# GpSimd's low parts moved, VectorE's first passes reordered, and two loops written out

## The reference

```python
# cross attention: 32 query heads, 8 key/value heads, head size 128
kv = concatenate([context, latents], axis=1)            # 256 rows per batch row
q, k, v = latents @ Wq, kv @ Wk, kv @ Wv                # q and k get an RMS norm per head
probs = softmax(q @ k.T / sqrt(128))
x = x + tanh(g_xattn[0]) * ((probs @ v) @ Wo)
# feed-forward, INTER = 1376, on layernorm(x) / 128
inter = silu(xf @ w_gate.T) * (xf @ w_up.T)
inter_q = trunc(clip(inter * 128, -128, 127))
x = x + tanh(g_ffn[0]) * trunc(clip((inter_q @ w_down.T) * 128, -128, 127))
```

## Time and profile before

| what | value |
| --- | --- |
| median of 3 runs | 1199.65 us (1199.49 to 1199.93) |
| the profiled execution | 1198.55 us, of which its span is 1196.8 us |
| TensorE busy (matmuls) | 1176.8 us, 98% |
| VectorE, ScalarE, GpSimd busy | 830.3, 580.5 and 326.9 us |
| TensorE clock granted | 1.000 over the span |

### The profile page before, as it was taken

How to read it: one execution, slowest core, us unless ns; L and a number is a source line. 1 busy time by engine, 2 the same in 40 slices (tenths; PEclk the granted TensorE clock), 3 DMA queues, 4 the chain that set the end, 5 groups by cost and what they waited for, 6 DMA issues and landing times.

```text
span 1196.8 us, 20842 instructions
## 1 busy us (share of the span) xinstructions
PE 1176.8 (98%) x6979; PEld 1008.7 (84%) x6979; DVE 830.3 (69%) x2402; ACT 580.5 (49%) x1352; POOL 326.9 (27%) x286
## 2 busy tenths in 40 slices
PE   8999999999999999999999999999999999999998
PEld 7888888888888888888988888888787777778786
DVE  6867677666766766667666667668877887875355
ACT  5645455454545455454554545554444445543432
POOL 4513022221303212031231203122342412225542
PEclk9999999999999999999999999999999999999999
DMA  7001010000101010010000000002122212583316
GB/s 281 12 25 54 1 37 18 36 33 2 53 0 35 18 35 35 0 53 0 35 19 33 35 0 0 1 1 56 32 80 79 81 54 71 204 321 100 108 44 246
DMA packets 36266, 69.65 MB, mean 58 GB/s; under 512 B 5858, under 2 KB 22242, under 8 KB 34166
## 3 DMA queue, kind: packets, MB, share of 16 engines
q1 hardware_dynamic: 30726, 56.65, 13.7%
q0 software_dynamic: 3760, 8.40, 2.2%
q10 hardware_dynamic: 1728, 3.93, 0.8%
HBM read 60.57 MB, written 12.32 MB: 61 GB/s over the span
## 4 chain that ended last, share of the span: by engine, by line
PE 60%; DVE 21%; issue 9%; ACT 5%; POOL 2%; DMA 2%; SPq 1%; DVEq 0%; ACTq 0%; POOLq 0%
PE bank L414 14%; PE bank L416 14%; PE bank L415 14%; PE bank L2274 5%; PE bank L2123 3%; DVE probs L1276 3%; ACT probs L881 2%; PE bank L1951 2%; PE bank L2286 2%; DVE iq L1475 2%; DVE k_junk L1231 2%; DVE row_max L1249 2%; DVE pt_lo L1263 2%; POOL k_rstd L648 1%; PE bank L1893 1%
## 5 line engine op out<-in xcount | busy, mean ns | idle before, releaser
L881 ACT ACTIVATE probs<-bank,exp_bias,q_rstd 128x256 f32<-128x256 f32 x256 | 141.1, 562 | 135.7 <-DVE exp_bias L1257 135.7
L1268 DVE TENSOR_TENSOR o_lo<-bank,o_hi 128x512 fp32r<-128x512 f32 x64 | 44.2, 691 | 175.6 <-ACT o_hi L874 175.6
L414 PE MATMUL bank<-wkv_hi,kv_src_lo 128*128 128x256 f32 x512 | 145.0, 283 | 0.7 <-DVE kv_src_lo L1318 0.7
L416 PE MATMUL bank<-wkv_hi,kv_src_hi 128*128 128x256 f32 x512 | 145.0, 283 | 0.0
L415 PE MATMUL bank<-wkv_lo,kv_src_hi 128*128 128x256 f32 x512 | 144.9, 283 | 0.0
L652 POOL TENSOR_TENSOR q_rstd<-q_var,minus_half 128x8 f32<-128x8 f32 x32 | 52.4, 1637 | 299.0 <-DVE q_var L1236 299.0
L870 ACT ACTIVATE pt_hi<-bank 128x512 fp32r<-128x512 f32 x128 | 69.6, 596 | 116.1 <-PE bank L1951 114.4
L414 PE MATMUL bank<-wo_hi,o_lo 128*128 128x512 f32 x256 | 104.2, 407 | 1.6 <-DVE o_lo L1268 1.2
L414 PE MATMUL bank<-wq_hi,kv_src_lo 128*128 128x512 f32 x256 | 103.2, 403 | 0.6 <-DVE k_lo L1218 0.6
L416 PE MATMUL bank<-wo_hi,o_hi 128*128 128x512 f32 x256 | 101.5, 396 | 0.0
L415 PE MATMUL bank<-wo_lo,o_hi 128*128 128x512 f32 x256 | 101.0, 394 | 0.0
(11 more groups left out here) (300 smaller groups left out, 3079.2 us busy)
## 6 DMA issues: line engine op xcount, KB each, us to landing
weights<-r_w SPq DMA_DIRECT2D x16, 768.0 KB, 9.7
wq_raw<-wq SPq DMA_DIRECT2D x8, 1024.0 KB, 4.8
wo_raw<-wo SPq DMA_DIRECT2D x8, 1024.0 KB, 4.8
wkv_raw<-wkv SPq DMA_DIRECT2D x8, 512.0 KB, 3.3
gu_raw<-w_gate SPq DMA_DIRECT2D x10, 256.0 KB, 3.4
gu_raw<-w_up SPq DMA_DIRECT2D x10, 256.0 KB, 3.7
wd_raw<-w_down SPq DMA_DIRECT2D x10, 256.0 KB, 3.8
y_back<-y_dram SPq DMA_DIRECT2D x5, 512.0 KB, 9.0
```

The costliest lines, as they stand in the source:

```text
L414: eng.matmul(out_ap, a_lo, b_hi, start=start, stop=False)
L416: return eng.matmul(out_ap, a_hi, b_hi, start=False, stop=stop)
L881: act.activation(probs[:, h, :], scores_ps[h // 2][:, (h % 2) * 256:(h % 2) * 256 + 256], ACT.Exp, bias=exp_bias[:, h:h + 1], scale=q_rstd ...
L1268: dve.tensor_tensor(o_lo[:, par, :], o_ps[:, :], o_hi[:, par, :].bitcast(F32), ALU.subtract)\
```

## The change

ScalarE's `wkv_high` of pass 5 stands ahead of the exponentials. GpSimd's `wkv_low` waits in addition for the bias of pass 5. GpSimd's `gu_low` is cut into two instructions, each for one of the two weights, and these and `wd_low` wait for steps of VectorE's work on the chunks; the counts of `gu_lo_ready` double, and SyncE drops one wait in its loop that the other covers. In the second pass of group 0 VectorE's order changes. `groups` and `chunks` are Python loops now, so every pass and chunk is written out.

```diff
--- before.py
+++ after.py
@@ -445,20 +445,14 @@
 
         def groups(eng, one_group):
 
-            one_group(0)
-            with eng.Fori(1, G - 1) as g:
+            for g in range(G):
                 one_group(g)
-            one_group(G - 1)
 
         def chunks(eng, one_chunk):
 
 
-            for j in range(2):
-                one_chunk(j, j, P, P)
-            with eng.Fori(1, (CH - 3) // 2) as i:
-                for j in range(2):
-                    one_chunk(i * 2 + j, j, P, P)
-            one_chunk(CH - 3, 0, P, P)
+            for c in range(CH - 2):
+                one_chunk(c, c % 2, P, P)
             one_chunk(CH - 2, 1, P, TAIL)
             one_chunk(CH - 1, 0, TAIL, 0)
 
@@ -531,10 +525,9 @@
             with sp.Fori(1, (CH - 1) // 2) as i:
                 for j in range(2):
                     c = i * 2 + j
-                    sp.wait_ge(gu_lo_ready, c - 1)
                     sp.wait_ge(wd_lo_ready, c - 1)
                     load_chunk(c, j, P)
-            sp.wait_ge(gu_lo_ready, CH - 2)
+            sp.wait_ge(gu_lo_ready, 2 * (CH - 2))
             sp.wait_ge(wd_lo_ready, CH - 2)
             load_chunk(CH - 1, 0, TAIL)
 
@@ -551,7 +544,7 @@
 
             load_context(0)
             load_context(1)
-            sp.wait_ge(gu_lo_ready, CH)
+            sp.wait_ge(gu_lo_ready, 2 * CH)
             sp.wait_ge(wd_lo_ready, CH)
             for e in range(SHARED):
                 sp.dma_start(s_raw[:, e, :], s_w[e, :, :]).then_inc(s_loaded, 16)
@@ -688,6 +681,7 @@
                     if before_end(g, b, 2) and not (isinstance(g, int) and g == 0 and b == 0):
                         k_root(next_pair)
                     if b == 4 and before_end(g, b, 4):
+                        pool.wait_ge(bias_ready, g * NB + 6)
                         wkv_low(g + 1)
                     if before_end(g, b, 2):
                         q_root(next_pair, (b // 2 + 1) % 2)
@@ -695,12 +689,10 @@
             groups(pool, one_group)
 
 
-            def gu_low(c, j, width):
+            def gu_low(c, j, i, width):
                 pool.wait_ge(gu_hi_ready, c + 1)
-                pool.tensor_tensor(gu_lo[:, j, :, :, 0:width].rearrange("p a c n -> p (a c) n"),
-                                   gu_raw[:, j, :, :, 0:width].rearrange("p a c n -> p (a c) n"),
-                                   gu_hi[:, j, :, :, 0:width].bitcast(F32).rearrange("p a c n -> p (a c) n"),
-                                   ALU.subtract).then_inc(gu_lo_ready, 1)
+                pool.tensor_tensor(gu_lo[:, j, i, :, 0:width], gu_raw[:, j, i, :, 0:width],
+                                   gu_hi[:, j, i, :, 0:width].bitcast(F32), ALU.subtract).then_inc(gu_lo_ready, 1)
 
             def wd_low(c, j, width):
                 pool.wait_ge(wd_hi_ready, c + 1)
@@ -711,13 +703,19 @@
 
             def next_low(c, j, width, following):
                 if following:
-                    gu_low(c + 1, 1 - j, following)
+                    if after_first(c):
+                        pool.wait_ge(iq_ready, c * 2)
+                    gu_low(c + 1, 1 - j, 0, following)
+                    pool.wait_ge(inter_step, c * 8 + 1)
+                    gu_low(c + 1, 1 - j, 1, following)
+                    pool.wait_ge(iq_ready, c * 2 + 1)
                     wd_low(c + 1, 1 - j, following)
 
             for t in range(3):
                 ln_root(NB + t)
             pool.wait_ge(probs_ready, 4 * (G * NB - 1))
-            gu_low(0, 0, P)
+            gu_low(0, 0, 0, P)
+            gu_low(0, 0, 1, P)
             routing_maps()
             for t in range(3, NB):
                 ln_root(NB + t)
@@ -939,13 +937,13 @@
                     if isinstance(g, int) and g == 0 and b == 1:
                         key_source_high(6)
                         key_source_high(7)
+                    if b == 5 and before_end(g, b, 3):
+                        wkv_high(g + 1)
                     exps(n, b)
                     if isinstance(g, int) and g == 0 and b == 1:
                         q_copy(next_pair)
                     if prev:
                         o_high(n - 1, (b - 1) % 2)
-                    if b == 5 and before_end(g, b, 3):
-                        wkv_high(g + 1)
                     if b % 2 == 0 and before_end(g, b, 2):
                         for half in range(2):
                             kv_high(next_pair, half, par)
@@ -1350,16 +1348,16 @@
                     if after_start(g, b, 3):
                         add_y(n - 3, (b - 3) % NB)
                     if isinstance(g, int) and g == 0 and b == 1:
-                        k_low(next_pair, par)
                         maxima(n)
                         bias_of(n, b)
+                        k_low(next_pair, par)
+                        pt_low(n - 1)
                         low_pair(3)
-                        pt_low(n - 1)
                         normalise(n)
                         q_norm(next_pair)
-                        o_low(n - 1, (b - 1) % 2)
                         for half in range(2):
                             q_low(next_pair, half, par)
+                        o_low(n - 1, (b - 1) % 2)
                         continue
                     maxima(n)
                     if after_start(g, b, 1):
@@ -2074,7 +2072,7 @@
 
             def inner_chunk(c, j, width, following):
                 if after_first(c):
-                    pe.wait_ge(gu_lo_ready, c + 1)
+                    pe.wait_ge(gu_lo_ready, c * 2 + 2)
                     inner_half(c, j, width, 0)
                 else:
                     pe.wait_ge(ln_lo_ready[0], 2 * NB)
@@ -2104,6 +2102,7 @@
             turn_x(5)
             inner_part_of(0, 0, P, 0, 0, 1, KC)
             turn_x(6)
+            pe.wait_ge(gu_lo_ready, 2)
             inner_part_of(0, 0, P, 0, 1, 0, 1)
             turn_x(7)
             inner_part_of(0, 0, P, 0, 1, 1, KC)
```

## The result

The changed kernel takes 1188.25 us (median of 4 runs, 1188.16 to 1188.85), the one before 1199.57 us in the same comparison (4 runs, 1198.79 to 1199.93): a ratio of 0.9905, interval 0.9889 to 0.992, so 9.6 to 13.3 us less. In a second comparison it was 1189.11 against 1199.99 us, ratio 0.9909 (0.9896 to 0.9923). The forecast was 1190.0 with a range from 1188.3 to 1193.2; the median lies 0.05 us under that range, and the forecast of 9.7 us less became 11.3 by these medians.

A forecast was written before the change was run, and what follows sets the result against it. TensorE, busy 98% of the span, was taken as the bound, so only its gaps could be won back. 6.2 + 1.0 + 2.7 - 0.2 = 9.7 us off the median 1199.65 gave 1190.0 us, range 1188.3 to 1193.2.

The forecast's parts named there:

- Passes b = 6: Attention loop: moving `wkv_hi` and `wkv_lo` earlier removes TensorE's 0.90 us stall in each of seven passes, 6.2 us gained.
- (b): Rival, attention: the stall in b = 6 stays in part; 1193.1 us with half won, 1196.2 with none; chance 0.10.
- (e): Rival, whole kernel: nothing moves, since another chain stands behind each of these waits; 1199 us, chance 0.03.
- Second pass of group 0: Start of attention: VectorE's new order lets TensorE start the scores earlier, 1.0 us gained, ends -0.8 and 2.0.
- Chunks: First feed-forward: VectorE's chunk falls from 11.5 to 10.3 us, under TensorE's 10.88; 2.7 us net gained.
- (a): Rival, chunks: TensorE waits for the new `gu_lo` as long as it waited for VectorE; 1192.6 us, chance 0.14.
- (c): Rival, chunks: the three GpSimd pieces block VectorE for their full length, making the kernel slower; 1208 us, chance 0.03.
- First `gu_lo` in two: Ahead of the chunks: two halves end slightly later and a VectorE bias may wait 0.25 us longer; 0.2 us lost.
- Loops: Attention and chunk loops written out: neither jump nor code fetching shows on TensorE's path; counted 0, ends ±0.3 us a group.
- (d): Rival, attention groups: fetching written-out code stalls TensorE 0.3 us a group over six groups; 1191.8 us, chance 0.03.
- I take the gain over to the median: Last step: the gain summed on the profiled execution (1198.55 us) is subtracted unchanged from the median, 1199.65 - 9.7 = 1190.0 us.

The follow-up runs named there:

- the late half: The changed kernel with the second half of `gu_lo` released by this chunk's first `iq`, about 3.3 us later than by the clip: 1199.31 us.

## Why the prediction was wrong, and where it was right

The mechanisms of the three moves were right, and the sum of their sizes was not: the step that failed is "6.2 + 1.0 + 2.7 - 0.2 = 9.7 us" with nothing for the loops. The stages gave 10.47 us. The largest error is VectorE's order in the second pass of group 0, put at 1.0 and measured at 1.31 us. Term by term:

*Passes b = 6*: 6.2 us predicted, 6.2 measured (0.82 + 0.88 + 5 x 0.90). The times within the pass came too: scaling expected at 304.86, found at 304.76 on the old scale; `q_lo` at 308.1 and 308.13. ScalarE's move alone does it, by the experiment. GpSimd's wait had no term of its own in the sum, and nothing is what it was worth. Rivals (b) and (e) are refuted.

*Second pass of group 0*: 1.0 predicted, 1.31 measured. The start of the second q tile was right (44.2, found 44.06 plus the 0.14 us by which this pass starts earlier), so was that of the values (47.05, found 46.91 plus 0.14). On the old scale the scores came at 50.57 and not 50.85. `q_lo` starts 1.32 us earlier and not 1.03: 0.6 us for `o_lo`, as said, and 0.7 because VectorE reaches the scaling that much earlier (46.51 plus 0.14, against 47.36), where the prediction left 0.4. VectorE no longer idles 0.56 us for `k_hi`. It is a size of a term.

*Chunks*: 2.7 predicted, 2.87 measured. VectorE's chunk was put at 10.3 us and is 10.2 (10.46 less 0.26 of waiting). Its three pieces cost 1.25 us where I had 1.35. The 0.2 us of loss in chunk 2 did not come: chunks 1, 2 and 3 start at 857.56, 868.44 and 879.32. Against the other profiles of before's chunks the gain is up to 3.2 us. Rival (a) is refuted for this order, but the late half shows that it is one step away. Rival (c) fell with the multiply at 906.82, undisturbed beside `gu_lo`. The Trainium skill, "SBUF — State Buffer", section "Who interferes with whom", says that a VectorE instruction with at most one SBUF input, outside the two-port modes, does not contend with GpSimd; that row agrees (one input from PSUM, 0.69 us). The same section of the Trainium skill has `tensor_scalar` able to enter a two-port mode and then contend; the clip at 907.54 is one, and it takes 0.67 us instead of 0.43 and ends 0.28 us after `gu_lo`.

*First `gu_lo` in two*: -0.2 predicted, about -0.1 measured, by the mechanism that was named. The last bias is held for 0.77 to 0.80 us in every profile with two halves and for 0.63 to 0.65 in every one with a single piece, and except in the run that reorders VectorE there, TensorE's pass in which it lies takes 6.75 to 6.78 us against 6.61 to 6.66.

*Loops*: 0 predicted. In the whole change they are worth 0.2 us (10.47 against 10.28), inside the stated ends. It lies in the last group, in the pass with the wait for `x_sb`: 9.25 us written out, 9.43 in loops. Alone the loops are worth 2.0; the prediction had seen their share on VectorE in the chunks and counted it there, and saw none in attention. Rival (d) is refuted: fetched instruction packets of queue 8 went from 30 to 57, and groups 1 to 6 take 102.53 us each.

The sum of the stages is thus 10.5 and not 9.7 us: 0.3 more in the second and third pass, 0.2 in the chunks, 0.2 by the loops, and 0.1 less lost by `gu_lo` in two. With 10.5 the same working gives 1189.2, which is inside the range.

The other 0.9 us went in the last step, "I take the gain over to the median", with "9 to 11" as the forecast's own range. It had no room for how executions differ. The median of before less that of the changed kernel is 11.3 us in one comparison and 10.9 in the other; the run with the end of attention reordered, whose stages are as long as the changed kernel's, gave 10.5 (1198.1 less 1187.63). Before's median itself was 1198.1, 1199.57, 1199.65 and 1199.99 us on different occasions. In the profiled spans the gain was 9.7 us: 10.47 in the stages, 0.14 ahead of them, and -0.88 in the second layer, by the delay among the routed experts. That this equals the forecast is luck, and so is which side of 1188.3 the median fell on: the same kernel had 1189.11 in the second comparison. What is left between 10.5 and 11.3 us is within the interval (9.6 to 13.3); up to 0.3 of it may be the chunks of before, which its first profile has at their shortest, and no run attributes the rest.

A slip beside the sum: the stated chances of all but (c) and (e) add to 0.94, and (e) has 0.03, where the prediction has 0.93 and 0.04.

## What to carry to other kernels

Look for an instruction that takes its length plus another engine's: here GpSimd's low parts held VectorE in mid-instruction, and TensorE's stall came 5 us later under another name. Move the producer into idle time ahead, or cut the long piece; the four waits that steered it here bought nothing that these runs show, and one placed one step late cost 11.9 us, more than all that was won. Savings by different means on one bound do not add: 2.0 us by the loops and 10.3 by the moves gave 10.5. And give a range at least the scatter of the executions, since a profile of each kernel can differ by 1 us in a place that the change doesn't touch.

## What was not expected of the hardware

Written-out code made attention 0.60 us shorter by itself: 0.4 in passes b = 6 (13.08 to 13.10 us for up to 13.16) and 0.2 in the last group. In pass b = 6 VectorE is no earlier. Group 2, the kernel before, and behind it the one with only the loops written out:

```profile
310.83 0.38 PE L414 MATMUL bank<-k_hi,q_lo 128*128 128x256 f32 x1 [0.64 <-DVE q_lo L1242]
```

```profile
309.07 0.39 PE L414 MATMUL bank<-k_hi,q_lo 128*128 128x256 f32 x1 [0.59 <-DVE q_lo L1236]
```

TensorE starts 0.83 us behind the start of `q_lo` in the loop (310.00) and 0.73 us behind it in straight code (308.34). What that time is made of no row shows. In the last group, straight code in both kernels, a pass of 9.44 us became 9.25; every profile with written-out loops has 9.24 to 9.26 (but for the one with a new order there), every one with loops 9.43 or 9.44, and no run explains it.

Two things vary between executions. The first transfer of `x` landed at 4.04 us in before's profile and at 5.46 in the changed kernel's. The changed kernel, VectorE's first instruction:

```profile
5.46 0.69 DVE L1169 BATCH_NORM_STATS2 ln_stats<-x_sb 128x6 f32<-128x512 f32 x1 [5.46 <-DMA x_sb<-x]
```

The second pass still started at 35.71 us against 35.85, so it was absorbed there; over 14 profiles it started between 34.20 and 35.85. The other is the delay of 0.9 us and more ahead of `g_silu`, in five of the 14 profiles and in either kernel. What releases it is named only "remote" in the profile, and no run here settled it.
